# Narrow attention: the last four heads' queries and keys projected side by side into one PSUM bank

## The reference, cut to what matters

```
stage 0, 1   attention, 20 heads of 64: on itself, then on the context    ("wide")
stage 2      feed-forward 320 -> 1280 -> 320 with GELU
stage 3, 4   attention, 20 heads of 16: on itself, then on the context    ("narrow")
stage 5      feed-forward
stage 6      two small gated attentions on 16 + 16 context tokens
stage 7      attention, 20 heads of 16, on the context                    ("narrow")
```

```
q = h @ Wq                 # h: layer-normed x (stage 7: x itself), 512 x 320
k = c @ Wk ; v = c @ Wv    # c: h in stage 3 ("own keys"), the context in stages 4 and 7
p = softmax(q_head @ k_head.T * 16 ** -0.5)      # each of 20 heads, 512 x 512
x = concat(p @ v_head) @ Wo + bo + x
```

## Time and profile before

| | |
|---|---|
| median of 3 runs | 3333.94 us (3331.95 to 3334.76) |
| profiled execution | 3336.34 us, span of its trace 3334.6 us |
| busy in the span | PE 3214.7 us (96%), DVE 1737.4 (52%), ACT 1476.5 (44%), POOL 805.1 (24%) |
| mean granted TensorE clock | 0.989 |
| chain that ended last | PE 89%, DVE 5%, ACT 4% |
| stages 3 and 4 | about 1780 to 2514 us of the span |
| stage 7 | about 2960 to 3334 us |

### The profile page before, as it was taken

One profiled execution on the slowest core, in us unless ns is written; L12 is line 12 of the kernel. 1 busy time (PEld: TensorE's weight loads), 2 busy tenths in 40 slices (PEclk: granted clock), 3 DMA queues, 4 the chain that ended last, 5 costly groups with the idle time before them and its releaser, 6 DMA issues.

```text
span 3334.6 us, 39289 instructions
## 1 busy us (share of the span) xinstructions
PE 3214.7 (96%) x15478; PEld 1462.8 (44%) x15478; DVE 1737.4 (52%) x2568; ACT 1476.5 (44%) x1983; POOL 805.1 (24%) x620
## 2 busy tenths in 40 slices
PE   7999999999999999999999999999999999989997
PEld 3344344443434343435444344444434545643443
DVE  2645455454555555552234677777762222656664
ACT  3544444445454545441112656666652112326664
POOL 2544444454554554550000000000000000000000
PEclk9999999999999999999999999999999999989999
DMA  3000000000100000000000000000002000000000
GB/s 110 24 16 20 16 17 20 23 19 20 58 18 18 17 23 13 16 24 20 0 5 26 1 1 1 30 11 6 1 23 65 1 0 33 1 5 6 14 9 17
DMA packets 37284, 62.32 MB, mean 19 GB/s; under 512 B 7024, under 2 KB 24944, under 8 KB 36208
## 3 DMA queue, kind: packets, MB, share of 16 engines
q1 hardware_dynamic: 37104, 59.82, 5.9%
HBM read 57.19 MB, written 2.62 MB: 18 GB/s over the span
## 4 chain that ended last, share of the span: by engine, by line
PE 89%; DVE 5%; ACT 4%; issue 1%; POOL 0%; DMA 0%; ACTq 0%; DVEq 0%; POOLq 0%
PE bank L1589 9%; PE bank L510 9%; PE bank L595 9%; PE bank L1126 7%; PE bank L737 5%; PE bank L351 5%; PE bank L673 5%; PE bank L1059 4%; PE bank L1251 3%; PE bank L676 3%; PE bank L709 3%; PE bank L1276 3%; PE bank L1179 2%; PE bank L533 2%; DVE heads L1084 2%; PE bank L1594 2%
## 5 line engine op out<-in xcount | busy, mean ns | idle before, releaser
L1084 DVE TENSOR_REDUCE heads<-bank 128x1 f32<-128x512 f32 x960 | 598.3, 683 | 237.2 <-PE bank L1072 236.4
L544 DVE TENSOR_REDUCE heads<-bank 128x2 f32<-128x1024 f32 x320 | 392.4, 1226 | 594.7 <-PE bank L533 594.7
L581 POOL TENSOR_TENSOR heads<-heads,probs 128x1024 f32<-128x1024 f32 x160 | 389.5, 2434 | 12.5
L567 ACT ACTIVATE probs<-bank 128x1024 f32<-128x1024 f32 x320 | 328.0, 1025 | 130.3 <-PE bank L519 130.0
L577 POOL TENSOR_TENSOR heads<-probs 128x1024 f32<-128x1024 f32 x80 | 190.7, 2384 | 712.8 <-ACT probs L567 712.8
L510 PE MATMUL bank<-heads 64*128 64x512 f32 x1280 | 335.7, 602 | 0.1
L1059 PE MATMUL bank<-heads 32*128 32x512 f32 x1920 | 296.8, 628 | 25.8 <-ACT weights L1097 10.9
L595 PE MATMUL bank<-probs,values 128*64 128x512 f32 x1280 | 294.0, 601 | 1.4 <-ACT nmT L558 1.0
L1589 PE MATMUL bank<-hT,weights 128*128 128x512 f32 x640 | 291.8, 606 | 1.5 <-issue 1.5
L1097 ACT ACTIVATE weights<-bank 128x1024 f32<-128x1024 f32 x236 | 228.8, 1022 | 96.0 <-PE bank L1059 93.9
L1652 ACT ACTIVATE ctx_in<-bank,b_col 128x512 f32<-128x512 f32 x80 | 55.1, 688 | 419.4 <-PE bank L1594 323.8
(11 more groups left out here) (205 smaller groups left out, 4868.9 us busy)
## 6 DMA issues: line engine op xcount, KB each, us to landing
heads<-in_wqk SPq DMA_DIRECT2D x40, 320.0 KB, 2.8
heads<-in_wqk SPq DMA_DIRECT2D x40, 256.0 KB, 2.6
weights<-in_L_xattn_w_ff SPq DMA_DIRECT2D x3, 1600.0 KB, 7.2
weights<-in_L_xattn_ff_w SPq DMA_DIRECT2D x3, 1600.0 KB, 7.1
ctx_in<-in_ctx SPq DMA_DIRECT2D x12, 384.0 KB, 3.7
weights<-in_L_xattn_qkv_q SPq DMA_DIRECT2D x2, 1632.0 KB, 7.4
weights<-in_L_xattn_wo SPq DMA_DIRECT2D x2, 1600.0 KB, 12.2
x_res<-in_x SPq DMA_DIRECT2D x4, 640.0 KB, 13.3
```

Source lines behind the costliest of these rows:

```text
L544: nc.vector.tensor_reduce(v["negm"][:, U % 2, qb, :].rearrange("p (g k) -> p g k", g=2)[:, :, 0], M.ROWS[:, :, :], AX.X, ALU.max, negate=T ...
L567: nc.scalar.activation(v["probs"][:, kb, :, :], M.COLS[kb % 2][:, :, :], ACT.Exp, scale=float(r.work[n][0].prm["dh"]) ** -0.5).then_inc(r. ...
L581: nc.gpsimd.tensor_tensor(ps, ps, pr[:, k, :, :], ALU.add).then_inc(r.sem("part"), 1)
L1084: nc.vector.tensor_reduce(v["negm"][:, tile, qb, 32 * h + at:32 * h + at + 1], r.bank_of(item, m)[:, :], AX.X, ALU.max, negate=True).then_ ...
```

## The change

Q2 and K2 become one item, QK2, in step 0. Six (five with a context) matmuls of 64 columns write q into partitions 0 to 63 and k into 64 to 127 of one bank, in turns. ScalarE copies the bank unmasked into a new place, M.tail (128 x 512, a free part of heads). GpSimd makes unit 4 from it: for Q and for K two masked copies of 64 rows (`tensor_scalar`, multiply and add), one of each two with a shift of 64 partitions, and then the cast as before. V3 moves from step 0 to step 2, where K2 was. Waits for K2 become waits for V3.

```diff
                 if i == 0 and now:
-                    items += [("Q2", n), ("V3", n)]
+                    items += [("QK2", n)]
...
                 if i == 2 and now:
-                    items += [("K2", n)]
+                    items += [("V3", n)]
...
             if c == 0:
-                r.wait_full(act, "K2", n - 1)
+                r.wait_full(act, "V3", n - 1)
...
+        def QK_pe4(pe, r, n):
+            s, v, bank = r.work[n][0], n_view(r, n), r.bank_of("QK2", n)
+            r.wait_free(pe, "QK2", n)
+            for e in range(3):
+                for home, name, x, ch in ((bank[0:64, :], "wq", M.hT, CH3), (bank[64:P, :], "wk", kvT(s), keys(s))):
+                    if e < len(ch):
+                        last = nc.tensor.matmul(home, v[name][0:ch[e][1], e, 256:320], x[0:ch[e][1], e, :], start=e == 0, stop=e == len(ch) - 1)
+            last.then_inc(r.full("QK2", n), 1)
+
+        def QK_act4(act, r, n):
+            r.wait(act, "q_tail", 2 * n)
+            r.wait(act, "k_tail", 2 * n)
+            r.wait_full(act, "QK2", n)
+            nc.scalar.copy(M.tail[:, :], r.bank_of("QK2", n)[:, :]).then_inc(r.free("QK2", n), 1)
+
+        def Q_tail_pool(pool, r, n):
+            v, low, high = n_view(r, n), slice(0, 64), slice(64, P)
+            r.wait(pool, "cols", 20 * n)
+            r.wait(pool, "q_cast", 5 * n)
+            r.wait_out(pool, "QK2", n)
+            r.wait(pool, "k_cast", 5 * n + 4)
+            for out, which in ((low, 0), (high, 1)):
+                r.wait(pool, "q_tail", 2 * n + which)
+                nc.gpsimd.tensor_scalar(v["QT"][out, 4, :], M.tail[low, :], M.mask[low, which:which + 1], M.mask[low, 6:7], ALU.mult, ALU.add
+                                        ).then_inc(r.sem("q_tail"), 1)
+            r.wait(pool, "q_tail", 2 * n + 2)
+            nc.gpsimd.tensor_copy(v["QB"][:, 4, :], v["QT"][:, 4, :]).then_inc(r.sem("q_cast"), 1)
+
+        def K_tail_pool(pool, r, n):
+            v, low, high = n_view(r, n), slice(0, 64), slice(64, P)
+            r.wait(pool, "q_cast", 5 * n + 5)
+            for out, which in ((low, 0), (high, 1)):
+                r.wait(pool, "k_tail", 2 * n + which)
+                nc.gpsimd.tensor_scalar(v["KT"][out, 4, :], M.tail[high, :], M.mask[high, which:which + 1], M.mask[high, 3 + which:4 + which],
+                                        ALU.mult, ALU.add).then_inc(r.sem("k_tail"), 1)
+            r.wait(pool, "k_tail", 2 * n + 2)
+            nc.gpsimd.tensor_copy(v["KB"][:, 4, :], v["KT"][:, 4, :]).then_inc(r.sem("k_cast"), 1)
...
                 if i == 0 and now:
-                    Q_pe4(pe, r, n, 2)
-                    V_pe4(pe, r, n, 3)
+                    QK_pe4(pe, r, n)
...
                 elif i == 2 and now:
-                    K_pe4(pe, r, n, 2)
+                    V_pe4(pe, r, n, 3)
...
                 if now:
-                    Q_pool4(pool, r, n, 2)
-                    K_pool4(pool, r, n, 2)
+                    Q_tail_pool(pool, r, n)
+                    K_tail_pool(pool, r, n)
```

More of the change, by code:

```diff
@@ L78, in __init__ @@
         self.QUAD = ctx.enter_context(nc.psum_tensor("bank0", [P, 4, 512], F32))
+        self.tail = self.heads[:, 10240:10752]
         self.pair = [self.QUAD[:, 0:2, :], self.QUAD[:, 2:4, :], ctx.enter_context(nc.psum_tensor("bank4", [P, 2, 512], F32))]
@@ L1258, in Q_act4 @@
             r.wait_full(act, item, n)
-            for u, which in ((2 * c, 0), (2 * c + 1, 1)) if c < 2 else ((4, 2),):
+            for u, which in ((2 * c, 0), (2 * c + 1, 1)):
                 last = nc.scalar.activation(v["QT"][:, u, :], r.bank_of(item, n)[:, :], ACT.Identity, bias=M.mask[:, 6:7],
@@ L1265, in Q_pool4 @@
             v = n_view(r, n)
-            r.wait_full(pool, f"row{min(2 * c + 1, 4)}_3_3", n - 1)
+            r.wait_full(pool, f"row{2 * c + 1}_3_3", n - 1)
             r.wait_out(pool, f"Q{c}", n)
-            for u in range(2 * c, min(2 * c + 2, 5)):
+            for u in range(2 * c, 2 * c + 2):
                 nc.gpsimd.tensor_copy(v["QB"][:, u, :], v["QT"][:, u, :]).then_inc(r.sem("q_cast"), 1)
@@ L1416, in narrow_steps_act @@
                 if i == 0 and now:
-                    Q_act4(act, r, n, 2)
-                    V_act4(act, r, n, 3)
+                    QK_act4(act, r, n)
                 if i == 1 and old:
@@ L1423, in narrow_steps_act @@
                 if i == 2 and now:
-                    K_act4(act, r, n, 2)
+                    V_act4(act, r, n, 3)
                 if i == 3 and feeds:
@@ L1557, in narrow_sync @@
                 elif b == 0:
-                    r.wait_full(sp, "K2", n - 1)
+                    r.wait_full(sp, "V3", n - 1)
                     load_weights(sp, s)
@@ L1567, in narrow_sync @@
             if r.then:
-                r.wait_full(sp, "K2", r.N - 1)
+                r.wait_full(sp, "V3", r.N - 1)
                 ff_load_first(sp, r.then)
```

## The result

The changed kernel takes 3311.68 us (median of 4 runs, 3311.16 to 3313.95) against 3334.35 us before (4 runs): ratio 0.9935, 95% interval 0.9923 to 0.9948, faster by 22.7 us. The forecast was 3310.4. Two later comparisons, on two chips, gave 0.9946 (0.9932 to 0.9960) and 0.9925 (0.9913 to 0.9938). Single executions of one and the same kernel, within one comparison, spread over 1.5 to 11 us.

What follows compares the result with a forecast made beforehand. TensorE was taken to set the pace, with a floor of about 3.3 us a step from the exponentials. Savings of 10.9, 5.9, 4.4 and 2.3 us, together 23.5, from the 3333.94 us median gave 3310.4 us; range 3305.5 to 3319.

Steps and rivals of the forecast that it cites:

- QK2 costs what Q2 cost: Step 0: the paired matmuls' two halves overlap, so QK2 takes about 2.75 us, Q2 took 2.84, and all of K2 goes.
- V3 out of step 0: Step 0 loses V3's full time on TensorE: 1.72 us with own keys, 1.18 us with context keys.
- Step 2 at its floor: Step 2, with V3 for K2, falls from 4.63 to 3.54 us (own keys) and 3.63 to 3.34 (context keys).
- Step 3: The step after V3's new place: some 0.1 us less in each batch, counted only in the range's fast end.
- the edge of the range: Fast end, 3305.5 us: step 2 with context keys loses its full 0.6 us, the next step some 0.1 a batch.
- ScalarE: One plain copy replaces two masked evictions (0.78 us for K2's) and V3's copy comes later, in idle time: no cost.
- GpSimd: Four added masked copies at 0.7 us, about 4.0 us with the casts, first read in step 10: no cost.
- Sum: Savings of 10.9 us (own keys), 5.9 (stage 4), 4.4 and 2.3 (stage 7): together 23.5 us.
- A: Rival: QK2's halves do not overlap and it takes up to 5.68 us; about 3338 us, no change; chance 6%.
- B: Rival: VectorE, the exponentials or row-bank waits in steps 3 and 4 give part back; 11 us saved, 3323; chance 9%.
- C: Rival: GpSimd's masked copies so slow (10 us each) that step 10 waits 3.2 us a batch; 3348 us; chance 3%.
- D: Rival: half tiles or shorter steps bring a granted clock of 0.50 into some batches, ten times 2 us; 3331; chance 3%.

## Why the prediction was right

- **QK2 costs what Q2 cost.** Worked out at 2.74 to 2.77 us, measured 2.80. That K's half is free is shown by leaving most of it out (2.79 us). The reason given, that the matmuls alternate, holds only in part: with context keys the other order costs 0.05 us, with own keys the alternation is worth 0.9 us a batch by the steps (the time of the whole kernel moved by 1.7 us only, within its uncertainty).
- **V3 out of step 0.** Worked out 1.72 and 1.18 us less; measured 5.67 to 4.01 (1.66) and 5.56 to 4.43 (1.13). The kernel with V3 back in step 0 shows that this is TensorE's own time.
- **Step 2 at its floor.** Taken from step 14 as 3.54 and 3.34 us; measured 3.53 and 3.34. The 4.63 us of the earlier trace rows for step 2 before was one batch's: the other own-keys batches had 4.49, so the gain is 0.96 us in a usual one, and the 1.0 of the sum was near it. The floor of the exponentials is shown by the same step without V3: 3.34 us too.
- **Step 3.** With context keys it also fell, 3.38 to 3.29 us, which only the edge of the range had. The two reasons given for that edge, 8 x 0.31 and 12 x 0.1 us, add up to 3.7 us and so to 3306.7, not 3305.5; nothing hangs on the difference.
- **ScalarE.** No cost, as said, but the margin was put too wide: the kernel with two copies shows 0.2 us.
- **GpSimd.** A masked copy was taken at 0.7 us and bounded by 2.4; it takes 0.76 to 0.78. The Trainium skill's 0.77 us (GPSIMD Engine Reference, section 3.1) was the nearer one; the trace agrees. Neither changed the sum, since 33 us are left to step 10, and 24 more copies cost nothing.
- **Sum.** 23.5 us worked out for the 12 batches, 23.9 us found in the two traces, 22.7 us between the medians. That it agrees so well has luck in it: the first own-keys batch gave 1.1 us, not 2.7. Its step 2 took 5.18 us at the lower clock in eight profiles (the changed kernel three times, K with one chunk, two copies on ScalarE, the wide mix in another order, and GpSimd's 24 and 48 copies), 3.53 us without alternation and with the earlier layer-norm, and 3.20 us with V3 in step 0. Stage 7's first batch gave 3.9 us, not 2.3, since less of it ran at that clock; a repeat of the changed kernel gained 7.1 us there. The two deviations cancel by luck.
- **Rivals.** A (halves do not overlap) is refuted by the pairs of records 0.01 us apart. B (part given back) did not come in the steps behind, which kept their times: steps 4 and 10 are 3.67 and 4.49 us as before. C (GpSimd late) has the place and the mechanism right, shown by the 48 copies, far from where the change is. D is what happened in one of the 12 batches, the first, for 1.6 us, in every profile of the changed kernel.

What stays open is why the clock falls in just that one step; no kernel was made for it. The traces point at the change itself: in the eight profiles the first batch's step 0 was short (4.65 to 4.82 us), while it took 6.49 us in the kernel before and with V3 in it and 5.35 us without alternation, and there step 2 kept its clock. With the earlier layer-norm step 0 was short too (4.01 us), but ran wholly at a clock of 1.00. That the short step 0 brings the fall is not shown.

## What to carry to other kernels

Measure each step from one fixed instruction to the next, and look for a step elsewhere in the same trace that already has the contents that the changed step will have; its length includes the floors that a sum of TensorE's instructions misses. Work that is taken from an engine-bound step and put into one at its floor is free or nearly so: V3 cost nothing in step 2 with context keys, and 0.2 us with own keys. And when an engine's share is 96%, the waits of 0.3 us that are left still add up: moving VectorE's short layer-norm writes out of steps 18 and 19, whose end held up the next reductions, gave another 5.6 us by steps and 9 us by the medians.

## What the runs showed of the hardware

In three orders of issue TensorE started matmuls for the other half of its columns ahead of their turn, by four records: with Q's six records ahead of K's, four of K's overlapped in both kinds of batch, and in the wide mix four of eight did (5.42 us for 16 records, 3.65 in turns). In the Trainium skill (TensorEngine Tiling (Array Packing), Key Properties) tiles operate independently; the trace agrees, with this reach as the limit. What sets it is open.

In and behind a stall of 9 us the granted clock was at 0.50, the lower of its two levels (1.2 and 2.4 GHz): step 10, with 4.3 us of it at that level, took 6.56 us instead of 4.49.
